# First batch of a gated cross-attention block: four units' probabilities added on VectorE, next input's rows moved to earlier units

## The chip, the cores and the metric

One NeuronCore of one Trainium2 chip runs the whole program. The metric is the time of the program on the device in microseconds, the median of three executions. Engines are named as in the profile: PE (TensorE, matrix products into PSUM), DVE (VectorE), ACT (ScalarE), POOL (GpSimd) and SP (SyncE, here only a queue that issues DMAs). They run side by side, each works through its own instructions strictly in order, and they wait for one another only at semaphores.

## What is computed

A block of cross-attention and a feed-forward part, for four inputs ("batches") of 512 rows and 512 columns, each with a context of 1024 rows. qdq rounds rows to int8 steps, with a scale of their own for each row.

```python
q = _qdq(layernorm(x)) @ _qdq(wq).T + bq            # 16 heads of 32
k, v = split(ctx @ wkv.T + bkv)
attn = softmax(q k^T / sqrt(32))                    # 512 x 1024, for each head
o = attn v
x = x + tanh(g_xattn) * (_qdq(o) @ _qdq(wp).T + bp)
h = layernorm(x)
x = x + tanh(g_ffn) * ((silu(h gate_w * gs) * (h up_w * us)) @ down_w * ds)   # weights as fp8 values
```

The softmax needs, beside the products of the probabilities with v, the sum of the probabilities of each row: its denominator.

## The kernel before

The batches run one after another (b = 0 to 3). The attention of a batch has 32 **units**: four groups g of four heads each, and in a group eight tiles t of 128 context rows (u = 8g + t). For a unit PE computes the scores of four heads (line 1674), ACT takes their exponential (line 927) into the ring `prob`, a part of the tensor r1, and PE multiplies the probabilities with v (`values`, line 1691), which gathers in one PSUM bank over the eight tiles. The denominators gather in another bank, DEN_BANK: `sums` (line 1705) multiplies the unit's probabilities by esel, whose one column of ones adds them over the 128 partitions.

In the batches after the first this is done otherwise for the first seven tiles of each group: DVE adds the probabilities of the tiles into the tensor acc (`add_unit`, line 1194; two instructions a unit, two heads each), and PE multiplies only the total by esel once for each group (`totals`, line 1715). `added(b, u)` says for which units; for these `values` itself counts p_used, which frees the slots, and ACT also waits for p_dve before it writes over a slot that DVE reads (in the loop around line 927). The ring holds three units there, and two units in the first batch (P_RING). In the first batch no unit is added on DVE: all 32 have their sums on PE.

In the first batch the units carry more, since the work that later batches do beside the feed-forward part of the batch ahead has to be done here:

- Units 0 to 21 (SINGLES = 22) go head by head, and in each of them PE computes a difference and a maxima product of a later group (lines 1579 and 1646), ACT keeps the difference (line 877, in two places: r1[:, 10:12] and fus), and DVE takes the maxima over it (line 1189). PE's next maxima product waits for DVE's last one (m_free). The maxima of a group are turned by PE (line 1601), clamped by DVE (line 1176, tile crow) and sent by SP as the shift row of the group (line 578); the first scores of the group wait for it. For the last group that is unit 24.
- The feed-forward weights are rounded to fp8 values in steps k of 128x512: SP loads, DVE makes the magnitudes (`w_magnitudes`, lines 1274 and 1277, one step in most units; steps 20 to 29 fall on units 22 to 31), POOL adds and subtracts them (lines 712 and 714). SP loads a step when POOL is through with the one that used its buffer. Steps 30 to 35 come later.
- After every second of steps 6 to 21 POOL splits a chunk of the next batch's context (lines 691 and 695) and loads another (line 682).
- The rows of the next input are normalised and scaled by DVE in pieces, the generator `x_ahead` (from line 1115 on): statistics (line 1069, two calls), aggregate (lines 1075 and 1077), normalised (line 1080, two), maxima of the rows (line 1046, two), scales and scaled rows (lines 1050 to 1055, two), raised for rounding (line 1061, two), and a last call that ends it. The inverse deviation between comes from POOL (line 701), behind the step W_VARIANCE. AHEAD_UNITS names the units in which a piece is called.
- In units 24 and 25 PE turns the projection weights (lines 1507 and 1635), and ACT copies them (lines 899 to 907).

What DVE issues in a unit, and in which order, stands in the loop of @block.vector: maxima, then one piece of x_ahead, then add_unit, then w_magnitudes. PE's order in a unit is: scores, values of the unit before, the mids (turns), sums of the unit before, difference and maxima.

Of the kernel before, what the change touches and what calls it, by code (L numbers as in the profile page):

```python
# [146 lines left out]
AHEAD_UNITS = ((11, 13, 15, 17, 19) + tuple(range(SINGLES, SINGLES + 8)), (3,) + tuple(range(8, 25)))  # L147
# [24 lines left out]
ADD_UNITS = [g * MT + t for g in range(G) for t in ADDED[g][1:]]  # L172
CTX_CHUNK = 128
# [18 lines left out]
W_VARIANCE = 16  # L192
# [81 lines left out]

def added(b, u):
    return b > 0 and u % MT in ADDED[u // MT]


def add_count(b, u, j):

    at = u + 1 if u % MT == 0 else u
    return ((b - 1) * len(ADD_UNITS) + ADD_UNITS.index(at)) * ADD_PARTS + j // ADD_HEADS + 1

# [53 lines left out]
def build(nc, ctxT, x, wq, wkvT, wp, gate_w, up_w, down_w, bqT, bkT, bv, bp, gsT, usT, ds,  # L337
          g_x, g_f, out):
    with ExitStack() as ctx:
# [92 lines left out]
        kept0 = (r1[:, 10:12, :], fus)  # L432
        kept1 = kst[:, 1, :, :].rearrange("p j m -> p (j m)").bitcast(F32).rearrange("p (s n) -> p s n", s=HG)
# [582 lines left out]
        def _(dve):  # L1016
# [177 lines left out]
            def add_unit(b, u):  # L1194

                if u not in ADD_UNITS:
                    return
                g = u // MT
                first = u % MT == ADDED[g][1]
                if first and g > 0:  # L1200
                    dve.wait_ge(acc_read, (b - 1) * (G - 1) + g)
                elif first:
                    dve.wait_ge(x_done, b * NT if b < B - 1 else b * NT - len(LATE))
                    dve.wait_ge(ctx_ready, min(b + 1, B - 1) * CHUNKS)
                for j in range(0, HG, ADD_HEADS):
                    sums, p = acc[:, j:j + ADD_HEADS, :], p_slot(b, u, j)
                    dve.wait_ge(exp_done, exp_count(b, u, j + ADD_HEADS - 1))
                    if first:
                        q = p_slot(b, u - 1, j)
                        other = prob[:, q:q + ADD_HEADS, :]  # L1210
                    else:
                        other = sums
                        dve.wait_ge(p_dve, add_count(b, ADD_UNITS[ADD_UNITS.index(u) - 1], j))
# [102 lines left out]
            for b in range(B):  # L1316
# [4 lines left out]
                for u in range(UNITS):  # L1321
# [8 lines left out]
                    if b > 0:  # L1330
                        add_unit(b, u)
# [170 lines left out]
        def _(pe):  # L1502
# [212 lines left out]
            def totals(b, g):  # L1715

                pe.wait_ge(p_dve, add_count(b, g * MT + ADDED[g][-1], HG - 1))
                for j in range(HG):
                    mm = nc.tensor.matmul(ps[j * DH:(j + 1) * DH, DEN_BANK, :], esel[:, g, :], acc[:, j, :],  # L1719
                                          start=False, stop=False)  # L1720
                if g < G - 1:
                    mm.then_inc(acc_read, 1)
# [57 lines left out]
            for b in range(B):  # L1780
                last = b == B - 1
                for u in range(UNITS):
# [14 lines left out]
                    if b > 0 and t == 0 and g > 0:  # L1797
                        totals(b, g - 1)
                values(b, UNITS - 1)
# [141 lines left out]
```

## Time and profile before

| | us |
|---|---|
| median of three runs | 902.94 |
| lowest and highest | 901.31, 903.01 |
| the profiled execution | 902.62 |
| its span, first to last instruction | 900.7 |
| TensorE's granted clock over it | 0.998 of full speed |

| engine | busy us | share | instructions |
|---|---|---|---|
| PE | 853.6 | 95% | 5174 |
| DVE | 679.1 | 75% | 1316 |
| ACT | 560.0 | 62% | 765 |
| POOL | 255.7 | 28% | 254 |

All times of the trace count from the start of the span. The attention of the first batch goes from about 71 to 181 us; units 22 to 31 begin at 148. A matmul in f32 is recorded as two, so eight records are four heads. Records of matmuls overlap, and of the instructions of DVE and ACT that stand behind one another the records overlap by some 0.06 to 0.1 us; the pitch of such instructions is therefore a little less than their durations.

### The profile page before, as it was taken

To read this page: it belongs to the slowest core of one execution; us is meant where nothing else is said; L and a number is where in the kernel's file an instruction comes from. 1 tells how busy PE (TensorE), PEld (TensorE's weight loads), DVE (VectorE), ACT (ScalarE), POOL (GpSimd) and SP (SyncE) were. 2 spreads that over 40 slices of the span, in tenths; PEclk is the share of its full clock that TensorE was granted. 3 is DMA by queue.
4 is the path that set the end of the run, shared out by engine and by line. 5 is a ranking of instruction groups with operands and counts; after the bars stand their busy time and mean duration, and the time that the engine had idled before them with its cause. 6 is when DMAs were issued, how large, how long until landed. Compare 5 with 4: busy or idle time off the path is not lost.

```text
span 900.7 us, 14105 instructions
## 1 busy us (share of the span) xinstructions
PE 853.6 (95%) x5174; PEld 333.1 (37%) x5174; DVE 679.1 (75%) x1316; ACT 560.0 (62%) x765; POOL 255.7 (28%) x254
## 2 busy tenths in 40 slices
PE   5999999999999999999899999999999989999998
PEld 2432222244333332234433332224433322224884
DVE  6988967989666788878666778986867868869322
ACT  5568988743456568772555649884356669972440
POOL 1337767862257400020018700002002210011230
PEclk9999999999999999999999999999999999999999
DMA  9335344221111332100111143300010024200001
GB/s 328 108 85 160 90 113 116 72 93 34 45 40 44 100 107 63 44 1 1 46 32 44 39 120 97 73 1 1 11 43 1 1 53 110 57 1 16 21 1 47
DMA packets 37253, 55.32 MB, mean 61 GB/s; under 512 B 8960, under 2 KB 15424, under 8 KB 37184
## 3 DMA queue, kind: packets, MB, share of 16 engines
q1 hardware_dynamic: 35264, 48.13, 18.7%
q0 software_dynamic: 1920, 6.29, 2.4%
q8 instruction: 41, 0.67, 0.3%
q14 instruction: 28, 0.23, 0.1%
HBM read 31.21 MB, written 4.19 MB: 39 GB/s over the span
## 4 chain that ended last, share of the span: by engine, by line
PE 66%; DVE 16%; ACT 8%; issue 7%; SPq 2%; DMA 1%; ACTq 0%; DVEq 0%
PE ps L1523 34%; PE ps L1711 8%; PE ps L1674 7%; PE ps L1691 6%; ACT r L927 5%; PE ps L1646 4%; DVE acc L1214 4%; PE ps L1705 3%; SPq L568 2%; PE ps L1719 1%; DVE r L1355 1%; DVE kst L1189 1%; DVE am L1046 1%; PE ps L1507 1%; DVE r L1055 1%
## 5 line engine op out<-in xcount | busy, mean ns | idle before, releaser
L927 ACT ACTIVATE r<-ps 128x1024 f32<-128x1024 f32 (+1 forms) x300 | 253.3, 902 | 53.5 <-PE ps L1674 51.1
L1189 DVE CUSTOM_DVE_ANT_0 kst<-ps,kst 128x512 f32<-128x512 f32 x192 | 124.5, 685 | 30.7 <-PE ps L1646 29.2
L1674 PE MATMUL ps<-qst,kst 97*128 97x512 f16 x512 | 137.4, 382 | 2.8 <-ACT r L927 1.0
L1691 PE MATMUL ps<-r,vv 128*32 128x512 f32 x1024 | 136.4, 604 | 3.4 <-ACT r L927 3.2
L1214 DVE TENSOR_TENSOR acc<-acc,r 128x1024 f32<-128x1024 f32 x120 | 138.7, 1216 | 0.0
L877 ACT ACTIVATE kst<-ps 128x1024 f32<-128x1024 f32 x96 | 98.1, 1022 | 54.6 <-PE ps L1579 54.3
L1523 PE MATMUL ps<-xs,w_up 128*128 128x512 f16 (+1 forms) x480 | 93.3, 337 | 0.0
L1523 PE MATMUL ps<-xs,w_gate 128*128 128x512 f16 (+1 forms) x480 | 93.2, 337 | 0.0
L1674 PEld LDWEIGHTS ps<-qst,kst 97*128 97x128 f16 x512 | 40.4, 97 | 138.6 <-ACT r L927 89.1
L1002 ACT ACTIVATE qst<-ps,gs_c 128x512 f32<-128x512 f32 (+1 forms) x60 | 36.1, 601 | 67.1 <-PE ps L1523 67.1
L1467 DVE SCALAR_TENSOR_TENSOR xq<-ps,us_c,qst 128x512 f32<-128x512 f32 (+1 forms) x60 | 38.6, 643 | 45.5 <-PE ps L1523 45.5
L1523 PE MATMUL ps<-ctx_hi,wkv_hi 128*128 128x512 f16 x128 | 49.8, 394 | 14.2 <-ACT ctx_hi L815 10.9
L1523 PEld LDWEIGHTS ps<-xs,w_gate 128*128 128x128 f16 x480 | 45.1, 98 | 36.2 <-issue 5.2
L1523 PEld LDWEIGHTS ps<-xs,w_up 128*128 128x128 f16 x480 | 44.0, 98 | 35.8 <-issue 8.2
L1579 PE MATMUL ps<-acc,q_reg 32*128 32x512 f16 x256 | 49.7, 384 | 3.9 <-issue 3.6
L1646 PE MATMUL ps<-k_reg,q_reg 32*128 32x512 f16 x256 | 49.6, 384 | 3.6 <-DVE mx L1189 2.9
L740 POOL TENSOR_TENSOR xres<-xres,bp_bc 128x512 f32<-128x512 f32 x12 | 14.9, 1270 | 129.7 <-ACT r L935 129.1
L701 POOL TENSOR_TENSOR rstd<-mv,mhalf 128x4 f32<-128x4 f32 (+1 forms) x9 | 10.3, 1145 | 139.7 <-DVE mv L1077 122.8
L1214 DVE TENSOR_TENSOR acc<-r 128x1024 f32<-128x1024 f32 x24 | 28.3, 1222 | 28.3 <-ACT r L927 28.3
L1523 PE MATMUL ps<-ctx_lo,wkv_hi 128*128 128x512 f16 x128 | 49.2, 389 | 0.3 <-DVE ctx_lo L1224 0.3
L1523 PE MATMUL ps<-wkv_hi,ctx_hi 128*128 128x512 f16 x128 | 48.7, 380 | 0.0
L1523 PE MATMUL ps<-ctx_hi,wkv_lo 128*128 128x512 f16 x128 | 48.6, 383 | 0.0
(182 smaller groups left out, 1388.1 us busy)
## 6 DMA issues: line engine op xcount, KB each, us to landing
kst<-k_reg SPq DMA_DIRECT2D x192, 64.0 KB
qst<-q_reg SPq DMA_DIRECT2D x192, 32.0 KB
xs<-in_x SPq DMA_DIRECT2D x4, 1024.0 KB, 5.9
cf<-in_ctxT POOLq DMA_DIRECT2D x16, 256.0 KB, 3.4
xres<-in_x SPq DMA_DIRECT2D x3, 1024.0 KB, 5.2
out<-xres SPq DMA_DIRECT2D x12, 256.0 KB, 2.0
acc<-in_down_w SPq DMA_DIRECT2D x10, 256.0 KB, 2.7
vv<-in_wkvT SPq DMA_DIRECT2D x2, 1024.0 KB, 9.8
```

What stands on the lines that cost most here:

```text
L877: nc.scalar.activation(kept(b, n), ps[:, first_bank:first_bank + 2, :], ACT.Relu, scale=2.0).then_inc(diff_kept, 1)
L927: nc.scalar.activation(prob[:, s:s + heads, :], ps[:, first_bank:first_bank + heads, :], ACT.Exp, scale=SCALE).then_inc(exp_done, 1)
L1002: nc.scalar.activation(tmp[:, i % 2, width], bank(d_bank(b, name))[:, width], ACT.Silu, scale=gs_c[:, tile:tile + 1]).then_inc(silu_done, 1)
L1189: ins = nc.vector.tensor_tensor_reduce(kept(b, n)[:, k, :], bank(PAIR + k), kept(b, n)[:, k, :], 1.0, -3.0e38, ALU.add, ALU.max, mx[:, g % ...
L1214: nc.vector.tensor_tensor(sums, other, prob[:, p:p + ADD_HEADS, :], ALU.add).then_inc(p_dve, 1)
L1467: nc.vector.scalar_tensor_tensor(out=fus[:, i % 2, width], in0=bank(d_bank(b, name))[:, width], scalar=us_c[:, tile:tile + 1], in1=tmp[:, ...
L1523: mm = nc.tensor.matmul(out, l, r, start=(k == 0), stop=(k == len(terms) - 1))
L1579: mm = nc.tensor.matmul(bank(first_bank + k), qhi[rows, g, i // 2 * P:(i // 2 + 1) * P], kdiff[rows, g % 2, :], start=True, stop=True)
L1646: mm = nc.tensor.matmul(bank(PAIR + k), qhi[rows, g, t * P:(t + 1) * P], khi[rows, g, 512:1024], start=True, stop=True)
L1674: mm = nc.tensor.matmul(bank(first_bank + k), kst[0:97, g % 2, j + k, t * P:(t + 1) * P], qst[0:97, g % 2, j + k, :], start=True, stop=True)
L1691: mm = nc.tensor.matmul(ps[j * DH:(j + 1) * DH, O_BANK, :], vv[:, t, h * DH:(h + 1) * DH], prob[:, p_slot(b, u, j), :], start=(t == 0), st ...
L1711: mm = nc.tensor.matmul(out[:, cols], f2_at(b, part, i)[:, t * P:(t + 1) * P], w_down[:, i, cols], start=(i == 0 and part == 0), stop=(i = ...
```

## The change

In the first batch the probabilities of the last group's first four tiles (units 24 to 27) are added on DVE, into acc0, which is r1[:, 8:12], the place in which differences were kept until unit 21. The first adds come in unit 25 (24 + 25), then 26 and 27, two instructions each. PE computes no sums for these four units, and multiplies the total by esel in unit 29, behind the sums of unit 28 (TOTAL0 = 5). ACT waits in units 26 to 29 for the add that reads the slot it writes over.

The pieces of x_ahead are called in units 10, 11, 12 and 14 to 22, in place of 11, 13, 15, 17, 19 and 22 to 29; there are eleven with work and the last one ends it, so nothing of it is left in units 22 to 29. POOL computes the inverse deviation behind step 14 in place of 16. In batches 1 to 3 nothing is changed.

```diff
--- before.py
+++ after.py
@@ -144,7 +144,7 @@
 D_BANK.append({n: _banks[k] if k < len(_banks) else (k + 1) % 8 for k, n in enumerate(D_SEQ[B - 1])})
 
 
-AHEAD_UNITS = ((11, 13, 15, 17, 19) + tuple(range(SINGLES, SINGLES + 8)), (3,) + tuple(range(8, 25)))
+AHEAD_UNITS = ((10, 11, 12) + tuple(range(14, 23)), (3,) + tuple(range(8, 25)))
 AHEAD_EARLY = (2, 2)
 STREAM0 = [s for n in A_SEQ0 for part in STEPS0.get(n, []) for s in part] + UNIT_LIST0
 assert [s for s in STREAM0 if s[0] == "D"] == DIFFS
@@ -170,6 +170,10 @@
 ADD_HEADS = 2
 ADD_PARTS = HG // ADD_HEADS
 ADD_UNITS = [g * MT + t for g in range(G) for t in ADDED[g][1:]]
+
+
+ADDED0, TOTAL0 = tuple(range(4)), 5
+ADD_UNITS0 = [(G - 1) * MT + t for t in ADDED0[1:]]
 CTX_CHUNK = 128
 CHUNKS = M // CTX_CHUNK
 
@@ -189,7 +193,7 @@
 W_NONE = (3, 6, 9, 11, 13, 15, 17, 19)
 W_UNITS = tuple(int(u not in W_NONE) for u in range(UNITS))
 WP_UNITS, WP_ROWS = (0, 1, 3, 4, 6, 7, 9), (6, 9)
-W_VARIANCE = 16
+W_VARIANCE = 14
 
 W_ALL = 28
 W_BUFFER = [k % (4 if k < W_ALL else 2) for k in range(W_STEPS)]
@@ -272,14 +276,24 @@
     return 2 * b + 3 if b < B - 1 else 2 * B
 
 
+def adds(b, g):
+
+    return ADDED[g] if b > 0 else ADDED0 if g == G - 1 else ()
+
+
 def added(b, u):
-    return b > 0 and u % MT in ADDED[u // MT]
+    return u % MT in adds(b, u // MT)
+
+
+def add_units(b):
+
+    return ADD_UNITS if b > 0 else ADD_UNITS0
 
 
 def add_count(b, u, j):
 
     at = u + 1 if u % MT == 0 else u
-    return ((b - 1) * len(ADD_UNITS) + ADD_UNITS.index(at)) * ADD_PARTS + j // ADD_HEADS + 1
+    return (sum(len(add_units(i)) for i in range(b)) + add_units(b).index(at)) * ADD_PARTS + j // ADD_HEADS + 1
 
 
 def p_slot(b, u, j):
@@ -430,6 +444,7 @@
         xqT = r1[:, 8:10, :].rearrange("p a n -> p (a n)").bitcast(BF16).rearrange("p (c n) -> p c n", c=CT)
         down = acc[:, 0:2, :]
         kept0 = (r1[:, 10:12, :], fus)
+        acc0 = r1[:, 8:12, :]
         kept1 = kst[:, 1, :, :].rearrange("p j m -> p (j m)").bitcast(F32).rearrange("p (s n) -> p s n", s=HG)
         f2 = r1[:, :, :].rearrange("p a n -> p (a n)").bitcast(F16).rearrange(
             "p (s t n) -> p s t n", s=2, t=FT)
@@ -1193,24 +1208,27 @@
 
             def add_unit(b, u):
 
-                if u not in ADD_UNITS:
+                if u not in add_units(b):
                     return
                 g = u // MT
-                first = u % MT == ADDED[g][1]
-                if first and g > 0:
+                first = u % MT == adds(b, g)[1]
+                total = acc if b > 0 else acc0
+                if first and b == 0:
+                    dve.wait_ge(m_free, FREE_AFTER[0, STREAM[-1]])
+                elif first and g > 0:
                     dve.wait_ge(acc_read, (b - 1) * (G - 1) + g)
                 elif first:
                     dve.wait_ge(x_done, b * NT if b < B - 1 else b * NT - len(LATE))
                     dve.wait_ge(ctx_ready, min(b + 1, B - 1) * CHUNKS)
                 for j in range(0, HG, ADD_HEADS):
-                    sums, p = acc[:, j:j + ADD_HEADS, :], p_slot(b, u, j)
+                    sums, p = total[:, j:j + ADD_HEADS, :], p_slot(b, u, j)
                     dve.wait_ge(exp_done, exp_count(b, u, j + ADD_HEADS - 1))
                     if first:
                         q = p_slot(b, u - 1, j)
                         other = prob[:, q:q + ADD_HEADS, :]
                     else:
                         other = sums
-                        dve.wait_ge(p_dve, add_count(b, ADD_UNITS[ADD_UNITS.index(u) - 1], j))
+                        dve.wait_ge(p_dve, add_count(b, add_units(b)[add_units(b).index(u) - 1], j))
                     nc.vector.tensor_tensor(sums, other, prob[:, p:p + ADD_HEADS, :], ALU.add).then_inc(p_dve, 1)
 
 
@@ -1327,8 +1345,7 @@
                         next(wp_parts, None)
                     if not last and u in AHEAD_UNITS[b > 0]:
                         next(ahead, None)
-                    if b > 0:
-                        add_unit(b, u)
+                    add_unit(b, u)
                     for _ in range(W_UNITS[u] if b == 0 else 0):
                         w_magnitudes()
                 if not last:
@@ -1714,11 +1731,12 @@
 
             def totals(b, g):
 
-                pe.wait_ge(p_dve, add_count(b, g * MT + ADDED[g][-1], HG - 1))
+                total = acc if b > 0 else acc0
+                pe.wait_ge(p_dve, add_count(b, g * MT + adds(b, g)[-1], HG - 1))
                 for j in range(HG):
-                    mm = nc.tensor.matmul(ps[j * DH:(j + 1) * DH, DEN_BANK, :], esel[:, g, :], acc[:, j, :],
+                    mm = nc.tensor.matmul(ps[j * DH:(j + 1) * DH, DEN_BANK, :], esel[:, g, :], total[:, j, :],
                                           start=False, stop=False)
-                if g < G - 1:
+                if b > 0 and g < G - 1:
                     mm.then_inc(acc_read, 1)
 
             def a_wait(name):
@@ -1796,6 +1814,8 @@
                         maxima(b, s)
                     if b > 0 and t == 0 and g > 0:
                         totals(b, g - 1)
+                    if b == 0 and u == (G - 1) * MT + TOTAL0:
+                        totals(0, G - 1)
                 values(b, UNITS - 1)
                 if b > 0:
                     totals(b, G - 1)
```

## Rows read from the trace of the kernel before

**Rows 1.** The page, busy time, share of the span and instructions
```profile
PE 853.6 (95%) x5174; PEld 333.1 (37%) x5174; DVE 679.1 (75%) x1316; ACT 560.0 (62%) x765; POOL 255.7 (28%) x254
```

**Rows 2.** Stretches: busy us (instructions) by engine, granted clock, DMA share, GB/s
```profile
161.40:174.00 12.60, 12.60 (x92) 3.25 (x91) 12.43 (x16) 9.34 (x11) 9.91 (x9) 1.00 0.22 64
...
174.00:181.40 7.40, 7.40 (x61) 1.90 (x58) 7.21 (x7) 3.88 (x4) 7.16 (x7) 1.00 0.23 70
```

**Rows 3.** Timeline of PE: start us, us, line, op, tiles, records
```profile
154.41 1.04 PE L1674 MATMUL ps<-qst,kst 97*128 97x512 f16 x4
...
170.21 1.04 PE L1705 MATMUL ps<-r,esel 128*32 128x512 f32 x8
...
171.18 1.04 PE L1674 MATMUL ps<-qst,kst 97*128 97x512 f16 x4
...
174.00 1.04 PE L1674 MATMUL ps<-qst,kst 97*128 97x512 f16 x4
```

**Rows 4.** The tile esel, all its matmuls of sums: ns min/median/max
```profile
L1705 PE MATMUL ps<-r,esel x352: 592/592/617, 76.2 to 807.0; 128*32 128x512 f32 x176
```

**Rows 5.** DVE's adds: all of line 1214, and eight in batch 1
```profile
L1214 DVE TENSOR_TENSOR acc<-acc,r x120: 1211/1216/1227, 329.1 to 804.4; 128x1024 f32<-128x1024 f32 x120
...
331.88 9.17 DVE L1214 TENSOR_TENSOR acc<-acc,r 128x1024 f32<-128x1024 f32 x8
```

**Rows 6.** Timeline of ACT, exponentials of unit 25
```profile
160.44 1.97 ACT L927 ACTIVATE r<-ps 128x1024 f32<-128x1024 f32 x2
```

**Rows 7.** All of line 1162, and timelines of DVE and POOL around two
```profile
L1162 DVE CUSTOM_DVE_ANT_0 acc<-k_reg x16: 672/681/1352, 42.3 to 700.8; 128x512 f16<-128x512 f16 x16
...
78.47 1.16 POOL L714 TENSOR_TENSOR w_gate<-xres 128x512 f16<-128x512 f32 x1
...
78.82 1.35 DVE L1162 CUSTOM_DVE_ANT_0 acc<-k_reg 128x512 f16<-128x512 f16 x1
...
226.83 1.15 POOL L714 TENSOR_TENSOR w_down<-acc 128x512 f16<-128x512 f32 x1
...
227.48 1.04 DVE L1162 CUSTOM_DVE_ANT_0 acc<-k_reg 128x512 f16<-128x512 f16 x1
...
227.94 1.60 POOL L712 TENSOR_TENSOR acc<-acc 128x512 f32<-128x512 f32 x1
```

**Rows 8.** DVE's scaling of rows: all of line 1055, and two at 158.87
```profile
L1055 DVE TENSOR_SCALAR xs<-xs,rs x16: 473/482/1384, 33.3 to 581.0; 128x512 f32<-128x512 f32 x16
...
158.87 2.49 DVE L1055 TENSOR_SCALAR xs<-xs,rs 128x512 f32<-128x512 f32 x2
```

**Rows 9.** POOL's last chunk, and DVE's magnitudes: ns min/median/max
```profile
161.04 1.22 POOL L691 TENSOR_TENSOR ctx_hi<-cf,zero 128x512 f16<-128x512 f32 x1
...
L1274 DVE TENSOR_SCALAR xres<-xres x14: 414/422/1376, 61.2 to 175.0; 128x512 uint16<-128x512 uint16 x14
...
L1277 DVE TENSOR_SCALAR xres<-xres x14: 293/295/1139, 61.7 to 175.4; 128x512 bf16<-128x512 bf16 x14
```

**Rows 10.** Timelines of DVE and POOL behind the units
```profile
184.18 0.69 DVE L1281 TENSOR_TENSOR vv<-ps,bv_bc 128x512 f32<-128x512 f32 x1 [2.66 <-PE ps L1523]
...
186.73 4.94 POOL L740 TENSOR_TENSOR xres<-xres,bp_bc 128x512 f32<-128x512 f32 x4 [0.59 <-DMA xres<-in_x]
...
190.42 1.28 DVE L1050 TENSOR_SCALAR sx<-am 128x4 f32<-128x4 f32 x1
```

**Rows 11.** DVE and SP in units 11 to 22; all of line 1080
```profile
114.75 1.28 DVE L1069 BATCH_NORM_STATS2 st<-xs 128x6 f32<-128x512 f32 x2
...
120.31 0.69 DVE L1189 CUSTOM_DVE_ANT_0 xq<-ps,xq 128x512 f32<-128x512 f32 x1 [1.42 <-PE ps L1646]
...
L1080 DVE TENSOR_SCALAR xs<-xs,mv,rstd x16: 536/543/1379, 24.7 to 561.8; 128x512 f32<-128x512 f32 x16
...
151.40 0.64 SPq L578 DMA_DIRECT2D qst<-crow  x1
```

**Rows 12.** The page, DMA issues: KB each, us to landing
```profile
out<-xres SPq DMA_DIRECT2D x12, 256.0 KB, 2.0
```

## The prediction

> **What bounds the kernel now.** I read the page first: TensorE (PE) is busy for 95% of the span, VectorE (DVE) for 75%, GpSimd (POOL) for 28% [rows 1]. Then the stretches of the first batch, because an average over the span says nothing of it. From 161.4 to 174.0, which is the end of unit 25 to the start of unit 30, PE is busy 12.60 of 12.60 us, DVE 12.43 and POOL 9.91; in the next 7.4 us it is 7.40, 7.21 and 7.16 [rows 2]. So PE sets the pace there, but DVE has no idle time to show for it and POOL little: the reader should see that three engines are full at once. The timeline of PE gives the places: scores of unit 24 at 154.41, sums of unit 27 at 170.21, scores of unit 29 at 171.18 and of unit 30 at 174.00 [rows 3]. A unit lasts 174.00 - 171.18 = 2.82 us. I take the start of unit 30's scores, 174.00, as the mark: all that the change does to units 24 to 29 shows as a shift of it, and from there to the end the order on PE is the old one.
>
> **What is taken from PE.** The sums of units 24 to 27 go, four times eight records (a matmul in f32 shows as two, 0.59 us each, four of them side by side [rows 4]). A group fills 171.18 - 170.21 = 0.97 us; the group of values ahead of it would then run into the next scores, where some 0.1 us of overlap is lost, so I take 0.9. One such group comes back as the totals in unit 29. Gross gain: 4 x 0.9 - 0.9 = 2.7 us, if PE remains what the others wait for.
>
> **What is put on DVE.** Three units (25, 26, 27) with two adds each, 128x1024 f32, both inputs in SBUF. The same instruction takes 1.21 to 1.23 us in the later batches, and eight behind one another take 9.17 us, so 1.14 us apart [rows 5]. Six are 6.9 us. By itself that would fit: the input rows that leave units 22 to 29 give more than that back. What matters is who waits. The ring of probabilities in the first batch is two units deep, so ScalarE's (ACT) exponentials of unit 28 wait for the adds of 26, those of 29 for the adds of 27, and those of 26 for the adds of 25; PE's totals in unit 29 wait for the last add. So from the first exponential of unit 25 to the totals there is one chain on DVE: two adds, the two magnitude instructions of step 23, two adds, those of step 24, two adds. Behind it lie PE's totals and, through the exponentials of 29, the second scores of unit 30.
>
> **When it begins.** The two exponentials of unit 25 run from 160.44 for 1.97 us [rows 6], and the first add can start behind the first of them, at 161.4. They are late already, since ACT copied the projection weights before them, and the change moves neither.
>
> **What an add costs beside POOL.** No add of before lies beside POOL's rounding, so I bound it. Lower end: 1.14 us, what it takes when POOL is idle [rows 5]. Upper end: the wait for one whole POOL instruction in front of each. The nearest rows are those of the key difference, the other DVE instruction with two SBUF inputs: its median is 0.68 us, but it takes 1.35 at 78.82, when POOL had begun an instruction of 1.16 us at 78.47, and 1.04 at 227.48 beside one begun at 226.83. And the POOL instruction that follows, recorded from 227.94, then takes 1.60 instead of 1.16: it waited in its turn [rows 7]. So the two engines exclude each other, whichever began first, and they take turns. That they take turns also where DVE's instructions stand back to back shows at 158.87: two scalings of 0.48 us each took 2.49 together, one POOL instruction ahead of each [rows 8]. The adds are nearer to these rows than to the lonely ones, if POOL has work. I therefore take the upper end.
>
> The Trainium skill (SBUF — State Buffer, "Who interferes with whom") has a rule that speaks against this change: a DVE instruction with two inputs in SBUF and a GpSimd one that reads SBUF exclude each other, and the second to issue is blocked for the whole of the first. The trace agrees [rows 7]. By the page the eight turns below would cost the full 1.16 us each, 9.3 us instead of 8.4; were the rule not to hold for a plain add, the first rival below would be the result.
>
> **Has POOL work then?** Yes. In the trace of before it starts the last context chunk at 161.04 [rows 9]. In the changed kernel DVE reaches its magnitudes of steps 20 to 22 early (nothing of the input rows stands between them), but step 19 a little later, so POOL goes from step 19 to 22 without a gap and is, by my count at 1.16 us an instruction, in step 21 at 161.4. From there it has ready: the rest of 21, one more instruction that ends it, two of the chunk, two of step 22, and two of step 23 and the first of 24 as soon as DVE has handed over their magnitudes. That is eight turns behind the partial one.
>
> **The chain summed.** Start 161.4; rest of the POOL instruction under way 0.5 (0 to 1.1); six adds 6.9; magnitudes of two steps, 0.42 and 0.29 us unblocked [rows 9], 1.4 in all; eight turns of POOL at 1.05 (1.60 less what it waited, from rows 7), 8.4. Last add at 178.6. Totals 0.9: scores of unit 30 at 179.5 instead of 174.0, so +5.5 us. With seven turns it is +4.4. I take +5.0: the 2.7 us gained on PE are inside, they are swallowed by the wait for the last add. The exponentials of 26 slip by under 1 us, those of 28 by about 1.5, those of 29 by 5; only the last is what PE sees in the end.
>
> **What comes behind.** After the last add DVE still has the magnitudes of steps 25 to 29, again in turns with POOL: 5 x 2.3 us, until 188 to 191, while the first value tile wants DVE at 184.18 + 5.2 in the moved time [rows 10]. 0 to 2 us. POOL's bias of the residual (186.73, 4.94 us) moves behind as well and can meet DVE's scaling of the outputs, where a tiny instruction already took 1.28 us at 190.42 [rows 10]: 0 to 1. I take 0.5 for both. Below nothing they can't go, since the same work is done later.
>
> **The input rows in units 10 to 21.** There are eleven pieces of work (the twelfth call only ends the generator), each issued between DVE's maxima and its magnitudes; they issue no DMA. DVE has 1.3 to 1.4 us of idle time before the maxima of such a unit [rows 11]. A pair of statistics or of maxima of the rows takes 1.28, the aggregate under 0.9, a scaled or normalised pair 0.9 to 1.1 unblocked and up to 2.5 where POOL's chunk is beside it (one takes 0.54 or 1.38) [rows 8, 11]. PE can wait for a unit's maxima some 1.5 us longer than now before it stops, as it has values and sums to do in between; the worst units, 15 and 19, come out 0.4 to 0.7 late, and the next have room. The deviation is asked for in unit 14 instead of 17; POOL is moved to compute it behind step 14 and has it about 2 us ahead, so the 0.6 us wait of before goes, which hid behind PE anyway. What is late next is the last shift row: its DMA is issued at 151.40 [rows 11], as soon as DVE has clamped it, and unit 24's scores need it at 154.41 [rows 3]. With one piece more in unit 21 and step 18 on POOL beside it, it comes 0.8 to 1.1 us later. A 256 KB store lands in 2.0 us [rows 12], so the row would be there at 154.5: a stall of 0.1, bounded by 0 and 1.5. I price this part at nothing; its cover is that one microsecond.
>
> **Sum.** 5.0 + 0.5 = +5.5 us. The profiled execution took 902.62 us, with a span of 900.7; the median of the three runs is 902.94, so 0.3 above it. 902.6 + 5.5 = **908.1 us**. About 0.2%, 1.8 us, is what a measurement of this kernel can tell from no change.
>
> **Rivals.** First, on the other side: POOL doesn't hold the adds. Then the chain loses its turns before adds (about six of the eight and the partial one), the last add is done by some 172.8, scores of unit 30 start at 171.3 to 173.8, and the time is 900.0 to 902.4. It decides where an add beside POOL takes 1.2 us instead of over 2. For it: the adds are a plain tensor_tensor, and no such one was seen beside rounding. Against it: rows 7, the same two inputs. Chance 0.22, of which 0.13 are below 901.1.
>
> Second: fewer turns, because DVE wins the ties or POOL waits for magnitudes: four turns less are 4.2 us less, 903.5 to 905. Against it are the 2.49 us of rows 8. Chance 0.08, half of it within 0.2%.
>
> Third: the shift row is later than I think, or the magnitudes behind cost their upper end. PE stops at 154.4 for 1 to 1.5 us, or DVE is 2 us late for the value tile: 909.5 to 911.5. Chance 0.08.
>
> Forecast: 0.62, with a range of its own from 906 to 910.5. Slower by over 0.2%: 0.62 + 0.04 + 0.08 = 0.74; within: 0.09 + 0.04 = 0.13; faster: 0.13. The range for 8 in 10 goes from 902.5 to 911.5: it leaves out the first rival's better part.
>
> **What would show it.** Right: six adds of which most are recorded with about 2.2 us, POOL instructions of 1.6 to 2.3 us between 161 and 179, PE idle before the totals and before the scores of 29 and 30 with the add or ACT named, scores of 30 near 179. Wrong: adds of 1.2 us, PE without a gap from 161 on, scores of 30 before 174. The part on the input rows is right if unit 24's scores still start at 154.4; a wait for the shift row there would prove it mispriced. What would upset the whole is POOL standing idle at 161.4, or the first add starting much later than the first exponential of unit 25.

## The result, and the profile after

The kernel after takes **905.43 us** (median of seven runs, 905.10 to 907.30), the kernel before beside it 902.27 (seven runs, 901.31 to 903.64): a ratio of 1.0034 with a 95% interval of 1.0025 to 1.0044. It is slower, by 3.2 us; the forecast was 5.5 slower. The profiled execution took 905.10 us, with a span of 903.0 and a granted clock of 1.000.

The page of after, busy time, share of the span and instructions, which answers to [rows 1]:

```profile
PE 850.2 (94%) x5150; PEld 331.8 (37%) x5150; DVE 688.6 (76%) x1322; ACT 560.3 (62%) x765; POOL 261.3 (29%) x254
```

PE is busy for 3.4 us less than before (853.6 against 850.2), and yet the whole takes longer. The stretch from the first add to the scores of unit 30, as in [rows 2]:

```profile
161.90:178.30 16.40, 10.63 (x68) 2.25 (x66) 16.12 (x11) 9.53 (x11) 15.78 (x9) 1.00 0.21 61
```

PE, which before was busy 12.60 of 12.60 us, is now busy 10.63 of 16.40; DVE is busy 16.12 and POOL 15.78 of it. Two engines are full, and PE waits for them; the busy time of DVE and POOL here holds their waits for one another, as the next timelines show. The first is that of DVE (r<-r on line 1232 are the new adds, lines 1292 and 1295 the magnitudes):

```profile
162.11 3.78 DVE L1232 TENSOR_TENSOR r<-r 128x1024 f32<-128x1024 f32 x2 [2.71 <-ACT r L942]
165.82 1.37 DVE L1292 TENSOR_SCALAR xres<-xres 128x512 uint16<-128x512 uint16 x1
167.22 1.14 DVE L1295 TENSOR_SCALAR xres<-xres 128x512 bf16<-128x512 bf16 x1
168.28 3.31 DVE L1232 TENSOR_TENSOR r<-r 128x1024 f32<-128x1024 f32 x2
171.52 1.37 DVE L1292 TENSOR_SCALAR acc<-acc 128x512 uint16<-128x512 uint16 x1
172.93 1.13 DVE L1295 TENSOR_SCALAR acc<-acc 128x512 bf16<-128x512 bf16 x1
173.98 3.31 DVE L1232 TENSOR_TENSOR r<-r 128x1024 f32<-128x1024 f32 x2
```

A pair of adds takes 3.31 instead of about 2.35 (two that are 1.14 apart, [rows 5]). The two instructions of a magnitude take 1.37 and 1.14, where their medians are 0.42 and 0.29 [rows 9]. That is not new: beside POOL they took as long in the kernel before, whose timeline of DVE has

```profile
165.33 1.38 DVE L1274 TENSOR_SCALAR xres<-xres 128x512 uint16<-128x512 uint16 x1
...
175.44 1.14 DVE L1277 TENSOR_SCALAR xres<-xres 128x512 bf16<-128x512 bf16 x1
```

but there PE waited for none of it (12.60 busy of 12.60 us). Now they stand between adds for which PE waits. The timeline of POOL in the kernel after:

```profile
162.79 2.02 POOL L706 TENSOR_TENSOR ctx_hi<-cf,zero 128x512 f16<-128x512 f32 x1
164.89 2.02 POOL L710 TENSOR_TENSOR ctx_lo<-cf,ctx_hi 128x512 f16<-128x512 f32 x1
166.98 1.22 POOL L727 TENSOR_TENSOR xres<-xres 128x512 f32<-128x512 f32 x1
168.28 2.23 POOL L729 TENSOR_TENSOR w_up<-xres 128x512 f16<-128x512 f32 x1
170.47 2.13 POOL L727 TENSOR_TENSOR xres<-xres 128x512 f32<-128x512 f32 x1
...
174.14 2.06 POOL L727 TENSOR_TENSOR acc<-acc 128x512 f32<-128x512 f32 x1 [0.23 <-DVE acc L1295]
```

Of the eight instructions that start between 162.79 and 176.28, six are recorded with 2.0 to 2.2 us instead of 1.16, and there is hardly a gap between them. At 168.28 an add and POOL's instruction start together: the add goes first, and POOL's record of 2.23 us holds the wait. And PE, as in [rows 3] (scores on line 1691, totals on 1737):

```profile
154.93 1.04 PE L1691 MATMUL ps<-qst,kst 97*128 97x512 f16 x4
...
167.00 0.61 PE L1691 MATMUL ps<-qst,kst 97*128 97x512 f16 x2 [1.32 <-ACT r L942]
...
172.71 0.60 PE L1691 MATMUL ps<-qst,kst 97*128 97x512 f16 x2 [1.45 <-ACT r L942]
...
177.34 1.06 PE L1737 MATMUL ps<-r,esel 128*32 128x512 f32 x8 [2.17 <-DVE r L1232]
178.34 1.04 PE L1691 MATMUL ps<-qst,kst 97*128 97x512 f16 x4
```

The 1.32 are in the middle of unit 27's scores, the 1.45 in the middle of unit 29's. The scores of unit 30 start at 178.34 instead of 174.00. Of these 4.34 us, 0.5 are there in the scores of unit 24 already (154.93 against 154.41). They were there at 44 us too, long before the first edit has work (DVE scales q on line 1150 at 44.26; the same instruction, now on line 1165, stands at 44.79). Executions differ by that much at the start: the second profile of the kernel before (e0 below) is 0.2 later than the first there, e1's 1.3. So **+3.8 us** arise between unit 24 and unit 30. Behind the units another 0.5 are added, as shown below, so the trace has +4.3 us for the change.

**Equal clocks.** The runs list a mean granted clock for each execution, and the time goes with it. Four groups of the kernel before, 75 executions, ran beside the experiments. 17 of them have 1.000; their medians by group were 901.48, 901.49, 901.18 and 901.70. With 0.998 they were 902.55, 903.00, 902.74 and 903.35, so a clock of 0.998 stands beside 1.1 to 1.7 us. The kernel after has 1.000 in five of its seven runs, median 905.19. At equal clocks the change costs 905.19 - 901.5 = **3.7 us**. The 901.5 comes from other groups than the 905.19: the clocks of the seven runs of before beside after are not on record. The 4.3 of the trace is one execution of each kernel, and the 0.6 between the two is less than single executions differ by (those of before with 1.000 go from 900.81 to 902.23). The difference of the medians is smaller still, which fits that more of after's executions kept the full clock. I give medians of either kind below, and say which.

### The profile page after: what moved, and what is told of

Its sections match the earlier page's. It is cut to its first block, busy times and chain, and to the rows that moved or that the text cites. A ratio compares the mean times of both kernels' runs of the same rounds, so it can differ in the third digit from the quotient of the medians.

```text
span 903.0 us, 14072 instructions
## 1 busy us (share of the span) xinstructions
PE 850.2 (94%) x5150; PEld 331.8 (37%) x5150; DVE 688.6 (76%) x1322; ACT 560.3 (62%) x765; POOL 261.3 (29%) x254
## 4 chain that ended last, share of the span: by engine, by line
PE 67%; DVE 17%; ACT 8%; issue 7%; DMA 1%; ACTq 0%; DVEq 0%
PE ps L1540 34%; PE ps L1728 8%; PE ps L1708 7%; PE ps L1691 7%; ACT r L942 5%; PE ps L1663 4%; DVE acc L1232 4%; PE ps L1722 3%; PE ps L1737 1%; DVE r L1372 1%; DVE r L1232 1%; DVE kst L1204 1%; DVE am L1061 1%; DVE r L1070 1%; PE ps L1524 1%
## 5 line engine op out<-in xcount | busy, mean ns | idle before, releaser
L1540 PE MATMUL ps<-wkv_hi,ctx_lo 128*128 128x512 f16 x128 | 48.5, 379 | 0.0
```

The costliest lines, as they stand in the source:

```text
L1540: mm = nc.tensor.matmul(out, l, r, start=(k == 0), stop=(k == len(terms) - 1))
```

## The experiments

e1 and e2 split the change in two. e3 and e4 shorten the instructions of POOL with which the adds take turns, in the changed kernel and in the one before. Cuts in the code are marked with three dots. All four ran beside one another.

**e1, the rows' part alone.** The adds of the first batch and their totals are off, the sums of units 24 to 27 are back.

```diff
-ADD_UNITS0 = [(G - 1) * MT + t for t in ADDED0[1:]]
+ADD_UNITS0 = []
...
 def adds(b, g):
-    return ADDED[g] if b > 0 else ADDED0 if g == G - 1 else ()
+    return ADDED[g] if b > 0 else ()
...
-                    if b == 0 and u == (G - 1) * MT + TOTAL0:
-                        totals(0, G - 1)
```

> The changed kernel without its adds: the input rows stay in units 10 to 22 and the deviation behind step 14, all 32 units have their sums on PE again. Theory (the loss comes from the adds taking turns with POOL): no adds, no loss, 902.3 us, within 0.7 of the kernel before; scores of unit 24 at the same place as before relative to unit 10. Rival (the rows overfill units 10 to 21, or make the shift row late): most of the 3.2 us stay, 904.5 to 905.5, and PE waits in units 15 to 24.

Measured: 900.48 us (ten runs), a ratio of 0.998 (0.997 to 0.9989). Moving the rows gains 2.1 us by the medians; at a clock of 1.000 it is 900.15 against 901.48, 1.3 us. I had priced this part at nothing. Units 10 to 31 are shifted by a constant 1.3 us against before, as everything from 71 us on is, so the gain isn't in the units. The timelines of DVE and POOL behind them show it:

```profile
186.26 4.96 POOL L755 TENSOR_TENSOR xres<-xres,bp_bc 128x512 f32<-128x512 f32 x4 [0.46 <-DMA xres<-in_x]
...
191.75 0.17 DVE L1065 TENSOR_SCALAR sx<-am 128x4 f32<-128x4 f32 x1
...
192.16 1.67 DVE L1070 TENSOR_SCALAR r<-r,rs 128x512 f32<-128x512 f32 x4
```

The tiny instruction takes 0.17 us here; before it took 1.28 beside POOL's bias [rows 10]. Before, the bias ended at 186.73 + 4.94 = 191.67, 1.25 behind the start of that instruction; here it ends at 191.22, 0.5 ahead of it. Without the rows between them DVE's magnitudes come sooner, so POOL is through with its steps sooner: 1.8 us, measured against that DVE instruction.

**e2, the adds alone.** The rows are back in their old units, and the deviation behind step 16.

```diff
-AHEAD_UNITS = ((10, 11, 12) + tuple(range(14, 23)), (3,) + tuple(range(8, 25)))
+AHEAD_UNITS = ((11, 13, 15, 17, 19) + tuple(range(SINGLES, SINGLES + 8)), (3,) + tuple(range(8, 25)))
...
-W_VARIANCE = 14
+W_VARIANCE = 16
```

> The kernel before with the adds alone: the input rows stay in units 11 to 19 and 22 to 29. Theory: the chain of DVE from unit 25 to the totals now also holds the pieces of rows of units 25, 26 and 27, each of two instructions that take turns with POOL, 2 to 3 us each, so 6 to 9 us more than the change, 911 to 914 us. Rival (the input rows are what costs, the adds save PE 2.7 us): 899.5 to 901.

Measured: 907.8 us (four runs), 1.0059 (1.0044 to 1.0074), 5.3 us slower. The sign and the cause held, the size was smaller than the 911 to 914 that I expected. The pieces of the rows stand ahead of the adds and between them, and PE's wait in front of the scores of unit 27 becomes 4.58 us:

```profile
164.92 1.77 DVE L1070 TENSOR_SCALAR xs<-xs,rs 128x512 f32<-128x512 f32 x2
166.61 3.30 DVE L1232 TENSOR_TENSOR r<-r 128x1024 f32<-128x1024 f32 x2
...
169.94 2.12 PE L1691 MATMUL ps<-qst,kst 97*128 97x512 f16 x4 [4.58 <-ACT r L942]
```

The first adds start at 166.61 instead of 162.11 (0.8 of it from the start). Four scores take 2.12 us instead of 1.04: behind that wait the clock was at its lower level.

**e3, the adds without POOL's turns.** Weight steps 21 to 24 are rounded by POOL on 4 of their 512 columns, and the last context chunk on one column. The rest of that work is left out. POOL sets places that then stay unwritten to zero, before step 17.

```diff
+W_SHORT = (21, 22, 23, 24)
...
+                n0 = 1 if b == 1 and c == CHUNKS - 1 else CTX_CHUNK
...
-                nc.gpsimd.tensor_tensor(w, w, mag, ALU.add).then_inc(w_step, 1)
+                n0 = 4 if k in W_SHORT else WCH
+                nc.gpsimd.tensor_tensor(w[:, 0:n0], w[:, 0:n0], mag[:, 0:n0], ALU.add).then_inc(w_step, 1)
...
```

> The changed kernel, in which POOL's instructions of steps 21 to 24 and of the last context chunk work on 4 columns or 1 instead of 512, so that they hold the ports for next to nothing (the weights and the context of those places are left unrounded and unsplit, a memset of zeros in an idle gap of POOL comes instead). Theory: adds take 1.2 us instead of 1.7 to 2.4, last add near 171, scores of unit 30 near 172 instead of 178.3, time 898.5 to 901. Rival (two-deep ring and DVE's own order bind, whatever POOL does): adds may be short but the scores of unit 30 stay at 176 to 178, time 904 to 905.5.

Measured: 899.56 us (six runs), 0.9966 (0.9952 to 0.998). The adds (here line 1243) and PE:

```profile
162.25 2.37 DVE L1243 TENSOR_TENSOR r<-r 128x1024 f32<-128x1024 f32 x2 [2.63 <-ACT r L953]
165.19 2.35 DVE L1243 TENSOR_TENSOR r<-r 128x1024 f32<-128x1024 f32 x2
168.12 2.36 DVE L1243 TENSOR_TENSOR r<-r 128x1024 f32<-128x1024 f32 x2
...
172.25 1.04 PE L1748 MATMUL ps<-r,esel 128*32 128x512 f32 x8
```

The first add starts as late as in after, but the last one is done at 170.48 instead of 177.29, and PE reaches the totals without a wait. The adds are as short as in the later batches [rows 5], with the same data, ring and waits. The turns with POOL are the price. From first to last add it is 8.2 us here and 15.2 in after. The adds give back 3.4 of the 7.0 us, and the two magnitudes between them 3.6: each takes 0.66 us here, from its start to the next add, and 2.46 in after.

**e4, the same shortening in the kernel before.** The edit is that of e3, and leaves the same work out. It is the base against which e3 is to be read.

> The kernel before with the same short instructions of POOL (same parts left out). PE has no gap there and waits for nobody, so both theories expect 901.5 to 902.5, at most 0.5 to 1 us less than the kernel before; it is the base for the run of the changed kernel with short POOL instructions. If it gained 3 us or more, the gain of that run would say nothing of the adds.

Measured: 900.66 us (ten runs), 0.9982 (0.9973 to 0.9992); that is 1.9 us less by the medians, and I had expected 901.5 to 902.5. As in e1, POOL is through sooner and its bias is out of DVE's way. Against e4, e3 gains 1.1 us by the medians, 1.5 at a clock of 1.000 (898.47 against 900.00, three and five runs). The traces have 1.4: in e3 the scores of unit 30 come that much sooner after those of unit 24 than in e4. So even with next to no turns the adds bring less than the 2.7 us that I took from PE's sums. In e3 PE still waits 0.25 and 0.47 us for ACT in units 26 and 27, and the scores of unit 29 take 1.36 us instead of 1.04.

**e5, other places for the magnitudes.** Step 23's and 24's are taken out of the chain: one step more in unit 24, none in 25 and 26, two in 28.

```diff
-W_UNITS = tuple(int(u not in W_NONE) for u in range(UNITS))
+W_UNITS = tuple(int(u not in W_NONE) + {24: 1, 25: -1, 26: -1, 28: 1}.get(u, 0) for u in range(UNITS))
```

> The changed kernel with the magnitudes of step 23 made in unit 24, ahead of the first add, and those of step 24 in unit 28, behind the last; nothing else stands between the six adds. Theory: the chain shortens by the two pairs of 2.5 us, last add near 173, scores of unit 30 near 173.6 instead of 178.3; but six steps are then left for units 28 to 31, and POOL's bias of the residual falls on DVE's scaling of the outputs, 3 to 4 us of it given back. 901.5 to 905, most likely 904. Rival (the adds' own waits bind, magnitudes fill gaps only): scores of unit 30 stay at 177 to 178, 905 to 906.

Measured: 908.6 us (four runs), 1.0065 (1.0049 to 1.0081): a miss, and on the other side. The chain itself got shorter: six adds in one row, and the scores of unit 30 at 176.08 instead of 178.34, with a start 0.4 us later than in after. That is less than I expected (near 173.6), since the six adds take turns with POOL as well: 12.50 us instead of 6.9. And it was lost again behind the units:

```profile
162.53 12.50 DVE L1232 TENSOR_TENSOR r<-r 128x1024 f32<-128x1024 f32 x6 [1.21 <-ACT r L942]
...
192.45 5.30 POOL L755 TENSOR_TENSOR xres<-xres,bp_bc 128x512 f32<-128x512 f32 x4 [0.76 <-DMA xres<-in_x]
...
193.99 4.44 DVE L1070 TENSOR_SCALAR r<-r,rs 128x512 f32<-128x512 f32 x4
...
201.13 1.86 PE L1524 MATMUL ps<-identb,r 128*128 128x128 bf16 x16 [4.96 <-ACT r L965]
```

POOL has the same work in the same time, so its bias starts no sooner than in after (192.45 against 192.03, all of it from the start), but the scaling does (193.99 against 196.02). So the scaling falls in the middle of the bias, and takes 4.44 us instead of 1.67. PE waits 4.96 us for it, and its clock goes down: 16 transposes take 1.86 us, where they take 1.05 at the full clock. The clock falls once more at 237.6 in this profile, whose execution is the longest of the four (909.48).

**e6, the totals later.** PE asks for the last add in unit 31.

```diff
-ADDED0, TOTAL0 = tuple(range(4)), 5
+ADDED0, TOTAL0 = tuple(range(4)), 7
```

> The changed kernel with PE's totals in unit 31 in place of 29, so that PE waits for the last add only through the exponentials of unit 29. If the ring of two binds as much as the totals (theory), the scores of unit 30 start in their second half at 178.3 as before and the totals cost their 0.9 us later, where nothing hides them: 905.5 to 906.5. If the totals' wait alone had bound, PE would gain: 903 to 904.5.

Measured: 905.7 us (five runs), 1.0039 (1.0025 to 1.0053), as expected no better than after. PE now waits for ACT instead, before both halves of unit 30's scores:

```profile
176.94 0.61 PE L1691 MATMUL ps<-qst,kst 97*128 97x512 f16 x2 [1.18 <-ACT r L942]
...
178.98 0.60 PE L1691 MATMUL ps<-qst,kst 97*128 97x512 f16 x2 [1.44 <-ACT r L942]
```

The totals aren't the only ones that ask for the last add. The exponentials of unit 29 write over the slots of unit 27 and wait for it too; a ring of two units leaves no slack. The second half starts at 178.98, with a start 0.6 us later than in after, where the scores began at 178.34. From 180.0 on the clock of this profile is at its lower level for a while, which adds to what the totals cost later. How much of the time each makes up was not separated.

**e7, two units instead of four.** One pair of adds is left.

```diff
-ADDED0, TOTAL0 = tuple(range(4)), 5
+ADDED0, TOTAL0 = tuple(range(2)), 5
```

> The changed kernel with only units 24 and 25 added on DVE (two adds in place of six, two groups of sums less, one of totals more). Theory: one pair of adds, 3.8 us beside POOL, delays the second exponentials of unit 26 by 0.5 to 1 us, PE saves 0.9 in all; with the 2.1 us that the run with the rows alone gained, 900.5 to 902.5. Rival (the loss is a fixed price of having adds at all, as the first chain starts late): 904 to 905.5.

Measured: 902.79 us (ten runs), 1.0001 (0.9991 to 1.001), 0.3 above the 900.5 to 902.5 that I expected. The one pair takes 3.76 us, and PE waits 0.48 and 1.32 us in unit 27's scores. In the trace the scores of unit 30 come 1.4 us later than before, counted from those of unit 24, and behind the units 1.0 is won, nearly as in e1. So what the rows' move gives and what the saved sums give (two groups less the totals) is eaten by one pair in turns with POOL.

**e0, the kernel before once more.** Its first profile has the clock at the lower level for a while from 229.0 on. This run asks whether that comes again.

> The kernel before, unchanged, for a second look at its trace. In the first one PE's granted clock is at the lower level from 229 to 232, behind a gap of 1.75 us, and costs some 1.2 us; the run with the rows alone, which has the same gap, doesn't show it. If the fall belongs to this kernel's timing it is here again, and the first instruction of the output scales (line 1050) again takes 1.28 us beside POOL. If it is chance, it is not here, and 1.2 us of what the rows alone seem to gain between two traces is none of their doing.

Measured: 902.57 us (one run), granted clock 0.996. The stretch in the first profile of the kernel before (the clock is the seventh value, behind the five engines):

```profile
226.00:240.00 14.00, 12.24 (x57) 4.46 (x55) 8.11 (x18) 5.58 (x8) 4.61 (x4) 0.88 0.29 67
```

In e0:

```profile
226.00:240.00 14.00, 12.24 (x57) 4.44 (x56) 8.11 (x18) 5.58 (x8) 4.45 (x4) 0.88 0.28 67
```

And in e1:

```profile
226.00:240.00 14.00, 12.23 (x64) 4.80 (x62) 9.47 (x21) 6.93 (x9) 4.86 (x4) 1.00 0.29 69
```

Twice the clock falls in this stretch in the kernel before (0.88), and it doesn't in e1 and in after (1.00). What is behind comes 1.7 us later where it falls: against the first profile of before, e1 is 0.2 us late at 215 us and 1.4 early at 323, and in after, e4 and e8 to e10 the same difference is 1.7 too. So the 1.2 us of the expectation was too small. The adds aren't what keeps the clock up: e1 has none.

**e8 to e10, the bias as a cost by itself.** In the kernel before (e8), in e1 (e9) and in the kernel after (e10) POOL adds the bias of the first residual on 4 of 512 columns, so the first batch lacks most of it.

```diff
-                    nc.gpsimd.tensor_tensor(residual(b, t), residual(b, t), bp_bc[:, :], ALU.add).then_inc(x_biased, 1)
+                    n0 = 4 if b == 0 else C
+                    nc.gpsimd.tensor_tensor(residual(b, t)[:, 0:n0], residual(b, t)[:, 0:n0], bp_bc[:, 0:n0],
+                                            ALU.add).then_inc(x_biased, 1)
```

> The kernel before with POOL's four bias instructions on the first input's residual (4.94 us from 186.7) working on 4 columns, so that the bias is left out for the rest. Theory (what the input rows gained by their move is that POOL ends sooner and its bias no longer stands in front of DVE's scaling of the outputs): the first look lost 1.1 us there and the second 0.7, the fall of PE's clock at 229 may go with it: 1 to 2.3 us less, 900.3 to 901.6. Rival (the move gains in units 10 to 31 themselves): 902.3 to 902.9, no change.

> The kernel with the rows alone moved, with the same short bias instructions. Theory: nothing is blocked there any more, so nothing is gained: 900.0 to 900.8, as with the rows alone (900.5). Rival (the bias costs something of its own wherever it lies): another 1 to 2 us less, 898.5 to 899.5.

> The changed kernel with the same short bias instructions. In its trace DVE's scaling of the outputs loses 0.85 us to one instruction of 1.02 in place of 0.17, and 0.75 to the four of 2.42 in place of 1.67, to POOL. Theory: 1.6 us less, 903.5 to 904.2; the rest against the rows alone, some 3.5 us, is the chain of adds. Rival (the adds' chain is all of it, the scaling is hidden): no change, 905 to 905.8.

Measured, ten runs each on one chip:

| | median us | ratio to before | with clock 1.000: median (runs) |
|---|---|---|---|
| before beside them | 902.99 | | 901.18 (5) |
| e8, before with a short bias | 900.26 | 0.9976 (0.9964 to 0.9987) | 899.93 (6) |
| e9, rows moved, short bias | 900.18 | 0.9971 (0.9959 to 0.9983) | 899.97 (8) |
| e10, after, short bias | 904.67 | 1.0017 (1.0005 to 1.0029) | 903.71 (5) |

e8 and e9 are the same, so with the bias out of the way the rows' move gives nothing more: its 1.3 us at equal clocks were the collision of bias and scaling. In their traces e1, e8 and e9 all win the same 1.1 us on the kernel before, behind the units. e10 against e9 is the price of the adds by themselves: 3.7 us at equal clocks, and 3.7 in the traces (the first value tile at 188.90 against 185.16, with starts that differ by 0.1). The medians give 4.5; five of e10's ten executions have a clock of 0.998 and only two of e9's. In after the collision is back, as POOL was held up by the adds:

```profile
192.03 4.94 POOL L755 TENSOR_TENSOR xres<-xres,bp_bc 128x512 f32<-128x512 f32 x4 [0.55 <-DMA xres<-in_x]
...
194.75 1.02 DVE L1065 TENSOR_SCALAR sx<-am 128x4 f32<-128x4 f32 x1
...
196.02 2.42 DVE L1070 TENSOR_SCALAR r<-r,rs 128x512 f32<-128x512 f32 x4
```

The tiny instruction takes 0.85 and the scaling 0.75 us longer than alone, 1.6 in all. In e10 they are gone: the tiny instruction takes 0.17, the scaling 1.68. Against after that is 905.19 - 903.71 = 1.5 us at equal clocks, and 0.8 by the medians; e10's median is 0.5 above the 903.5 to 904.2 that I expected.

**e11, POOL waits.** The work is complete here: POOL does step 21, stands still until the last add, and goes on; its bias waits until DVE has scaled the outputs.

```diff
+                    if k == 21:
+                        pool.wait_ge(p_dve, len(ADD_UNITS0) * ADD_PARTS)
...
+                pool.wait_ge(oy_ready, NT)
                 residual_bias(0)
```

> The changed kernel with two waits more on POOL, nothing left out: behind step 21 it waits for the last add, before it splits the last context chunk, and its bias of the first residual waits until DVE has scaled the outputs. Theory: the adds take 1.2 us each as with the short POOL instructions, scores of unit 30 start near 173.2, DVE's scaling isn't blocked. POOL has eight rounding steps and the chunk left at 171, some 22 us, so it ends at 194 and its bias at 199, about when the first projection wants it (near 199): 899 to 900.7, no worse than the rows alone and possibly 1 us better. Rival (POOL can't afford the pause): DVE waits at its last magnitudes or for the bias, 1 to 4 us are lost, 901.5 to 905.

Measured: 905.7 us (ten runs), 1.0036 (1.0024 to 1.0047): a miss, on the side of the rival and 0.7 above its 901.5 to 905. The adds are short, and the scores of unit 30 start at 173.76, sooner than in the kernel before (174.00). But the pause costs elsewhere (timeline of POOL, of DVE, of PE):

```profile
171.09 1.16 POOL L706 TENSOR_TENSOR ctx_hi<-cf,zero 128x512 f16<-128x512 f32 x1 [8.16 <-DVE r L1235]
...
178.62 1.11 DVE L1295 TENSOR_SCALAR xres<-xres 128x512 uint16<-128x512 uint16 x1 [6.22 <-DMA xres<-in_up_w]
...
199.24 1.87 PE L1527 MATMUL ps<-identb,r 128*128 128x128 bf16 x16 [5.39 <-ACT r L968]
```

POOL's rounding frees the buffers into which SP loads the next weight steps. With POOL 8.16 us late the loads are late; DVE stands idle 6.22 us for one of them, makes the remaining magnitudes in turns with POOL until 188.2, and only then turns to the first value tile, which could have been there some 4 us sooner. PE waits 5.39 us and restarts at the lower clock. POOL has no slack of that size in the first batch.

## Why the prediction was right, and where it was off

- **Sign and mechanism: right.** DVE's adds and POOL's rounding exclude each other and take turns; the first rival (POOL doesn't hold the adds) fell with the timelines above and, on the same data, with e3. The measured 905.4 lies just below the forecast's own range of 906 to 910.5, and just above the second rival's 903.5 to 905 (fewer turns): a part of that rival came true, as the next point shows. The Trainium skill's rule (SBUF — State Buffer, "Who interferes with whom"), that an instruction of DVE with two inputs in SBUF and one of GpSimd that reads SBUF lock each other out for a whole instruction, holds for these plain adds: they are 1.14 us apart alone, and a pair takes 3.31 (3.30 to 3.32 in e2, e6 and e10 too). The price of a turn was not the whole 1.16 us of POOL's instruction that the prediction worked out from it, but 0.9.
- **The chain: the turns were too many and too long.** The prediction's sum was 17.2 us from first to last add: 0.5 partial, 6.9 adds, 1.4 magnitudes, eight turns of 1.05. Measured are 162.11 to 177.29, 15.2 us. The partial wait is 0.5 (3.78 - 3.31 for the first pair), and adds and magnitudes stand as summed, so 6.4 are left for turns. POOL's timeline has seven instructions that start and end in between, not eight: 0.9 us each. The eighth, "one more instruction that ends it" (step 21), was already under way when the first add came (POOL began it at 161.67), and the sum had it as the partial wait and as a turn besides. The first adds of the second and the third pair weren't blocked: at 168.28 add and POOL start together and POOL waits, and ahead of the last pair POOL itself had to wait for the magnitude in front of the add ([0.23 <-DVE acc L1295] at 174.14). The forecast stood on 7.5 turns of 1.05, 7.9 us: 1.5 too many. The later start and the totals give 0.3 back, which leaves the 1.2 between the +5.0 forecast for the chain and the +3.8 measured.
- **The mark and the waits: mostly right.** PE is idle before the totals with the add named (2.17) and in unit 29's scores with ACT named (1.45), and the scores of 30 start at 178.34, which was to be near 179. Before the scores of 30 themselves there is no wait, and the prediction had none in unit 27, where PE waits 0.49 and 1.32 us: the exponentials of 26, which were to slip by under 1 us unseen, are what it waits for there. The start was 161.6 without the 0.5 of the start-up, against 161.4.
- **What is taken from PE: right in size, wrong in worth.** PE's busy time falls by 3.4 us, not far from the 2.7 gained, but with the turns gone only 1.1 to 1.5 us reach the end (e3 against e4).
- **The shift row: right.** Unit 24's scores still start where they did, 0.5 late with everything else; no wait stands there. The row's DMA is issued at 152.84 instead of 151.40, 0.9 later without the start, where 0.8 to 1.1 was forecast. The deviation's wait is gone too.
- **The rows' part "at nothing": wrong, and right in the sum by luck.** Alone it gains 1.3 us at equal clocks (2.1 by the medians), because POOL's steps end sooner and its bias leaves DVE's scaling alone (e1, e8, e9). I looked only at what the pieces press on in their new units, not at who moves up where they leave. Beside the adds the gain doesn't show: they delay POOL by more than the rows gave it. Nothing in the prediction said so.
- **The tail, +0.5: about right.** DVE's magnitudes did not delay the value tile beyond the shift (188.51 against 184.18, 4.33). The collision of bias and scaling costs 1.6 us in after, where the kernel before had 1.1 of it: +0.5.
- **The sum.** 3.8 + 0.5 by the trace, 3.7 at equal clocks, 3.2 by the medians, against +5.5. What turns 3.7 into 3.2 is probably the clock: 17 of 75 executions of before kept 1.000, five of seven of after. But the clocks of the seven runs beside after are not on record, and that the difference comes from the change is not shown. The two spans differ by only 2.3 us (903.0 and 900.7): the profile of before has the fall of the clock at 229, 1.7 us, and 0.9 us behind 535, which the profiles of most other runs don't have.

**Open.** What decides whether the clock falls at 226 to 240 was not found: it did in the profiles of before, e0, e5 and e7, and in none of the other ten. Of all executions, 30 of 50 kept 1.000 in e1, e4 and e8 to e10, one of ten in e7. The profiles start up to 1.4 us apart and keep that difference, so times from two of them are to be compared between two marks, and totals only with that in mind.

The complete version that beats both kernels is e1: the rows moved and no adds, 900.48 us, 0.998 of the kernel before.

## What to carry to other kernels

Before work goes from a full TensorE to VectorE, look at GpSimd in the same stretch: here an add with two SBUF inputs that takes 1.14 us alone cost about 0.9 us more for every GpSimd instruction in its way, and so did the small instructions between the adds, which took about half of what the turns cost (e3). A ring of two slots handed the delay to TensorE at once, and shifting the wait (e6), the neighbours (e5) or GpSimd (e11) only moved it, to a place where the pause was long enough to cost clock as well. And a part that is priced at nothing should be asked what it frees, not only what it presses on: here the half that gains lay in that.

## What the runs showed of the hardware

- After a wait of PE of 4.58, 4.96 and 5.39 us the granted clock was at the lower of its levels (1.2 instead of 2.4 GHz): 2.12 us instead of 1.04 for four scores, 1.86 and 1.87 instead of 1.05 for 16 transposes. After the waits of 1.45 and 2.17 us in the kernel after it was not. It also fell behind waits as short as these: in e6 at 180.0, behind 1.45, 1.18 and 1.44 us, and in the kernel before at 229.0, behind one of 1.75.
- Where two instructions exclude each other, the size of one says little of its recorded time. In e3 POOL adds 4 columns just after DVE has begun an add; its timeline:

```profile
165.35 1.11 POOL L732 TENSOR_TENSOR xres<-xres 128x4 f32<-128x4 f32 x1 [3.25 <-DVE xres L1306]
```

The same instruction takes 0.20 us at 161.62, where DVE is idle, and 0.30 to 0.38 in e4, where no add is beside it; most of the 1.11 is the wait for DVE's.
